# Two places in TensorE's order: a score ahead of the last stack transposes, and a score between the halves of the values

## Chip, core and metric

One core of a Trainium2 chip. The metric is the device time of one execution in microseconds (us). The kernel before takes 53.62 us, the median of 3 runs (53.51 to 53.62).

## What is computed

The input x is (2, 128, 16, 16): two batches, 128 channels, 256 positions. A recurrent layer over the channels comes first, then an attention layer over 256 tokens of 128 features, and a table-like layer at the end. The change concerns the attention:

```python
qkv = jnp.einsum('bsh,oh->bso', x, w_qkv)
qkv = qkv.reshape(batch, seq_len, 3, nh, hd)          # 8 heads of 16
q, k, v = jnp.transpose(qkv, (2, 0, 3, 1, 4))
attn = jnp.einsum('bhqd,bhkd->bhqk', q, k) / math.sqrt(hd)
pos = jnp.arange(seq_len)[None, :] - jnp.arange(seq_len)[:, None]
bias = jnp.where(pos <= 0, pos.astype(jnp.float32) * math.log(RECENCY_DECAY), jnp.zeros((), dtype=jnp.float32))
attn = jax.nn.softmax(attn + bias[None, None, :, :], axis=-1)
out = jnp.einsum('bhqk,bhkd->bqhd', attn, v).reshape(batch, seq_len, hidden)
return jnp.einsum('bsh,oh->bso', out, w_out) + b_out
```

## The kernel before

Each engine runs an order written out by hand; semaphores join them. There are 2 batches of 8 heads, which makes 16 heads h, in 4 groups g of 4 heads. Steps named here are functions of the same name in the blocks of the engines.

**Stacks.** Queries and keys are split into high and low f16 parts, duplicated, and transposed on TensorE by `transpose_stacks(g)` (eight 128x128 transposes, L935). They go to one bank of PSUM (bank 6 for groups 2 and 3), and ScalarE (`even_stacks(g)`, L488) and VectorE (`odd_stacks(g)`, L668) copy them out. `transpose_stacks(3)` waits until both have copied group 2.

**Maxima.** `scores_by_query(h)` (L963) makes the scores of head h with queries on the partitions, two f16 matmuls of 128x256, into one of two banks in turn. VectorE's `largest(h)` (L761) takes their maxima, and after the fourth head of a group writes them as two f16 parts (L768, L769). `scores_by_query(h)` waits until `largest(h - 2)` is over. `shift_rows(g)` (L977) transposes the parts, and `even_shifts(g)` on ScalarE (L492) and `odd_shifts(g)` on VectorE (L672) put them into rows of the stacks.

**Probabilities and values.** `scores_by_key(h)` (L994 and L996, four matmuls) makes the shifted scores with keys on the partitions. ScalarE's `exponentials(c)` (L511) takes two heads at once. `values(g, t)` (L1013) multiplies the probabilities of the four heads of a group by the values, for half t of the keys: eight f32 records of 128x32 with 256 columns, one head beside the other in the array, and half 1 adds to half 0. Both halves wait for `exponentials(2g + 1)`. Values(0) and values(1) wait for more: values(0) until stacks 3 are copied out of the bank, values(1) for `by_query(0)`. Half 1 releases VectorE.

**Normalisation.** VectorE transposes the result (`by_query(g)`, L679), inverts the sums (`invert(g)`, L683), GpSimd multiplies (L352), VectorE transposes back (`by_dim(g)`, L687), and TensorE projects (`project(b)`, L1029). VectorE's order around the change is: largest(5), odd_stacks(2), largest(6), largest(7), odd_stacks(3), largest(8), odd_shifts(1), largest(9), by_query(0), largest(10), invert(0), largest(11), largest(12), by_dim(0), odd_shifts(2), largest(13), by_query(1), invert(1), largest(14), by_dim(1), largest(15), residual(0). ScalarE's is even_stacks(2), exponentials(0), even_stacks(3), exponentials(1), even_shifts(1), exponentials(2), exponentials(3), even_shifts(2), and so on.

TensorE's own order stands at the end of its block; behind the loop come project(0), shift_rows(3), values(2, 0) and (2, 1), four scores by key, values(3, 0) and (3, 1), and the tail.

Of the kernel before, what the change touches and what calls it, by code (L numbers as in the profile page):

```python
# [23 lines left out]
HG = 4  # L24
# [17 lines left out]
def conv_attn_ffn(nc, x, log_A, dt_w, dt_b, ln_w, ln_b, w_qkv, w_out, b_out, out):  # L42
# [3 lines left out]
    with ExitStack() as ctx:  # L46
# [781 lines left out]
        def _(pe):  # L828
# [94 lines left out]
            def transpose_stacks(g):  # L923

                b = g // 2
                pe.wait_ge(s_dup, HALVES * (b + 1))
                pe.wait_ge(s_hi1, HALVES)
                if g >= 2:
                    pe.wait_ge(s_even0 if g == 2 else s_even, 2)
                    pe.wait_ge(s_odd0 if g == 2 else s_odd, 2)  # L930
                for o in range(2):
                    for a in range(2):
                        for t in range(HALVES):
                            h = HG * (g % 2) + 2 * a
                            last = pe.transpose(stacks_ps[g][:, o, a, P * t:P * (t + 1)],  # L935
                                                parts[:, 2 * b + t, o, h:h + 2, :, :]
                                                .rearrange("p h i d -> p (h i d)"), ident16[:])
                last.then_inc(s_stacks, 1)
# [10 lines left out]
            def scores_by_query(h):  # L949

                b, e = h // HEADS, h % HEADS
                if h < HG:
                    pe.wait_ge(s_even0, h // 2 + 1)
                    pe.wait_ge(s_odd0, h // 2 + 1)
                else:
                    pe.wait_ge(s_even, h // HG)
                    pe.wait_ge(s_odd, h // HG)
                if h == 0:
                    pe.wait_ge(s_pad, 7)
                if h >= 2:  # L960
                    pe.wait_ge(s_max, h - 1)
                for t in range(HALVES):
                    last = pe.matmul(s1_ps[h % 2][:, HW * t:HW * (t + 1)],  # L963
                                     qT[:, e, HW * b + P * t:HW * b + P * (t + 1)],
                                     kT[:, e, HW * b:HW * (b + 1)], start=True, stop=True)
                last.then_inc(s_s1, 1)

            def shift_rows(g):

                pe.wait_ge(s_mp, g + 1)  # L970
                if g == 0:
                    pe.wait_ge(s_woT, 1)
                else:
                    pe.wait_ge(s_mre, g)
                    pe.wait_ge(s_mro, g)
                for t in range(HALVES):
                    last = pe.transpose(mT_ps[:, P * t:P * (t + 1)],  # L977
                                        mparts[:, g, t, :, :].rearrange("p h w -> p (h w)"), ident16[:])
                last.then_inc(s_mT, 1)

            def scores_by_key(h):

                c, b, e = h // 2, h // HEADS, h % HEADS
                pe.wait_ge(s_mre if h % 2 == 0 else s_mro, h // HG + 1)
                if h % 2 == 0:
                    if c >= 2:
                        pe.wait_ge(s_exp, c - 1)
                    else:
                        pe.wait_ge(s_lo, HALVES * (c + 1))
                        pe.wait_ge(s_v, HALVES * (c + 1))  # L990
                        pe.wait_ge(s_consts, 2)
                for t in range(HALVES):
                    dst = s2_ps[c % 2][:, h % 2, HW * t:HW * (t + 1)]
                    pe.matmul(dst, kT[:, e, HW * b + P * t:HW * b + P * (t + 1)], qT[:, e, HW * b:HW * (b + 1)],  # L994
                              start=True, stop=False)
                    last = pe.matmul(dst[:, P * t:HW], ident16[:], qmk[:, 0:HW - P * t], start=False, stop=True)  # L996
                if h % 2 == 1:
                    last.then_inc(s_s2, 1)

            def values(g, t):  # L1000

                b = g // 2
                if g == NG - 1:
                    pe.wait_ge(s_mre, NG)
                    pe.wait_ge(s_mro, NG)
                elif g > 0:
                    pe.wait_ge(s_pvq, g)
                else:
                    pe.wait_ge(s_odd, NG - 1)
                    pe.wait_ge(s_even, NG - 1)  # L1010
                pe.wait_ge(s_exp, 2 * g + 2)
                for j in range(HG):
                    last = pe.matmul(pv_ps[g][VW * j:VW * (j + 1), :],  # L1013
                                     v_aug[:, 2 * b + t, HG * (g % 2) + j, :], probs[:, HG * g + j, t, :],
                                     start=(t == 0), stop=(t == HALVES - 1))
                if t == HALVES - 1:
                    last.then_inc(s_pv, 1)
# [62 lines left out]
            scores_by_key(0)  # L1080
            scores_by_key(1)
            scores_by_query(6)
            scores_by_key(2)
            transpose_stacks(3)
            scores_by_query(7)
            scores_by_key(3)
            for g in range(2, NG):
                scores_by_query(HG * g)
                shift_rows(g - 1)
                scores_by_query(HG * g + 1)  # L1090
                values(g - 2, 0)
                values(g - 2, 1)
                scores_by_query(HG * g + 2)
                scores_by_key(HG * g - 4)
                scores_by_key(HG * g - 3)
                scores_by_query(HG * g + 3)
                scores_by_key(HG * g - 2)
                scores_by_key(HG * g - 1)
# [42 lines left out]
```

## Time and profile before

| | |
|---|---|
| median of 3 runs | 53.62 us (53.51 to 53.62) |
| the profiled execution | 53.42 us |
| its span in the profile | 51.7 us |
| busy in the span: TensorE | 40.9 us (79%) |
| VectorE | 40.2 us (78%) |
| ScalarE | 28.6 us (55%) |
| GpSimd | 23.5 us (45%) |
| the chain that ended last: TensorE, VectorE, GpSimd, ScalarE | 35%, 24%, 13%, 10% of the span |

A row of the timeline gives the start from the span's beginning and the duration in us, the engine (PE is TensorE's matmuls, DVE VectorE, ACT ScalarE, POOL GpSimd), the line, the operation, what it writes and reads with shapes, and how many instructions are merged; in brackets stands the idle time of the engine before it, and what ended it. The chain of work that ended last is followed back from the last instruction; "issue" in it is time in which nothing in the profile explains the wait. Matmuls overlap: the distance of two starts is what one takes from the engine, and the recorded duration is longer.

### The profile page before, as it was taken

How to read it: one execution, taken by the hardware profiler on the slowest of the kernel's cores; microseconds unless marked ns; L12 is line 12 of the kernel's file. 1: busy time of each engine (PE TensorE's matmuls, PEld its weight loads, DVE VectorE, ACT ScalarE, POOL GpSimd, SP SyncE). 2: the span in 40 equal slices, each digit the busy share in tenths (PEclk: the TensorE clock that was granted, in tenths of full speed). 3: DMA queues.
4: the chain of work that ended last, by engine and by line, in shares of the span. 5: the costliest groups of instructions: out<-in, count | busy, mean ns of one | idle time of the engine just before them, and what ended most of it. 6: DMA issues, size and time to landing. Idle time of an engine off the chain costs nothing.

```text
span 51.7 us, 1021 instructions
## 1 busy us (share of the span) xinstructions
PE 40.9 (79%) x310; PEld 26.3 (51%) x312; DVE 40.2 (78%) x135; ACT 28.6 (55%) x63; POOL 23.5 (45%) x64
## 2 busy tenths in 40 slices
PE   0999899999996859649957996999994596996700
PEld 0332789685442645429824682599482352842500
DVE  2799778848983599999889999989999954699520
ACT  3600656395476768967998079339649900056020
POOL 4789432099999989736950031040029204016000
PEclk9999995569999999999999999999999999999999
DMA  0392400000000000000000000000000000002002
GB/s 0 80 304 42 35 5 0 0 0 0 0 0 6 0 0 0 0 6 13 6 0 0 0 0 0 0 13 0 0 0 0 0 0 0 0 0 101 1 0 101
DMA packets 1565, 0.92 MB, mean 18 GB/s; under 512 B 404, under 2 KB 1560, under 8 KB 1560
## 3 DMA queue, kind: packets, MB, share of 16 engines
q1 hardware_dynamic: 1104, 0.79, 4.9%
q10 hardware_dynamic: 456, 0.08, 1.7%
q8 instruction: 2, 0.03, 0.3%
q14 instruction: 3, 0.02, 0.2%
HBM read 0.60 MB, written 0.26 MB: 17 GB/s over the span
## 4 chain that ended last, share of the span: by engine, by line
PE 35%; DVE 24%; POOL 13%; ACT 10%; issue 7%; DMA 6%; POOLq 0%; DVEq 0%
PE ps L1013 8%; ACT probs L511 8%; DMA x_sb<-in_x_dram 6%; PE ps L994 5%; PE ps L963 4%; POOL stacks L303 4%; DVE negmax L761 4%; POOL stacks L304 4%; PE ps L996 4%; PE ps L935 3%; PE ps L1029 3%; PE ps L859 2%; POOL parts L310 2%; PE ps L913 2%; POOL wc L298 2%
## 5 line engine op out<-in xcount | busy, mean ns | idle before, releaser
L761 DVE TENSOR_REDUCE negmax<-ps 128x2 f32<-128x512 f32 x16 | 10.7, 675 | 0.8 <-PE ps L963 0.6
L511 ACT ACTIVATE probs<-ps 128x1024 f32<-128x1024 f32 x8 | 8.0, 1021 | 3.9 <-PE ps L996 3.9
L833 PE MATMUL ps<-warm 128*128 128x512 bf16 x28 | 8.9, 452 | 1.4 <-DVE warm L556 1.3
L994 PE MATMUL ps<-stacks 128*128 128x256 f16 x32 | 7.0, 273 | 0.0
L352 POOL TENSOR_TENSOR on<-pvq,rsum 128x256 f32<-128x256 f32 x3 | 1.8, 616 | 10.7 <-DVE rsum L683 10.7
L996 PE MATMUL ps<-qmk,ident 128*128 128x256 f16 (+1 forms) x32 | 6.6, 246 | 0.0
L963 PE MATMUL ps<-stacks 128*128 128x256 f16 x32 | 6.0, 274 | 0.2 <-ACT stacks L485 0.2
L833 PEld LDWEIGHTS ps<-warm 128*128 128x128 bf16 x30 | 3.2, 113 | 5.0 <-issue 2.2
L1013 PE MATMUL ps<-probs,v_aug 128*32 128x256 f32 x64 | 4.3, 384 | 1.7 <-ACT probs L511 1.5
L913 PE MATMUL ps<-wT,xtT 128*128 128x384 f32 x8 | 3.2, 505 | 0.7 <-ACT xtT L437 0.6
L994 PEld LDWEIGHTS ps<-stacks 128*128 128x128 f16 x32 | 3.1, 98 | 0.8 <-ACT stacks L492 0.4
L1013 PEld LDWEIGHTS ps<-probs,v_aug 128*32 128x32 f32 x64 | 1.9, 108 | 3.1 <-issue 2.0
L963 PEld LDWEIGHTS ps<-stacks 128*128 128x128 f16 x32 | 2.5, 97 | 2.0 <-issue 1.3
L996 PEld LDWEIGHTS ps<-qmk,ident 128*128 128x128 f16 x32 | 3.1, 98 | 0.2
L498 ACT ACTIVATE fln<-fmv 128x2 f32<-128x2 f32 x2 | 0.4, 203 | 5.1 <-DVE fmv L712 5.1
L488 ACT COPY stacks<-ps 64x1024 f16<-64x1024 f16 x3 | 3.0, 1005 | 0.3 <-PE ps L935 0.3
L935 PE MATMUL ps<-ident,parts 128*128 128x128 f16 x32 | 2.3, 219 | 0.8 <-POOL parts L310 0.8
L1029 PE MATMUL ps<-woutT,oT 128*128 128x128 f32 x16 | 2.5, 289 | 0.4 <-DVE oT L687 0.4
L1029 PEld LDWEIGHTS ps<-woutT,oT 128*128 128x128 f32 x16 | 2.0, 191 | 1.3 <-issue 1.3
L935 PEld LDWEIGHTS ps<-ident,parts 128*128 128x128 f16 x32 | 1.8, 97 | 1.6 <-issue 1.0
L977 PE MATMUL ps<-ident,mparts 128*128 128x128 f16 x8 | 1.1, 224 | 1.8 <-DVE mparts L769 1.8
L687 DVE STREAM_TRANSPOSE oT<-on 128x256 f32<-128x256 f32 x4 | 1.8, 443 | 0.9 <-POOL on L360 0.7
(159 smaller groups left out, 94.4 us busy)
## 6 DMA issues: line engine op xcount, KB each, us to landing
x_sb<-in_x_dram SPq DMA_DIRECT2D x1, 256.0 KB, 2.9
out_dram<-y_sb SPq DMA_DIRECT2D x2, 128.0 KB, 1.7
wqkv_sb<-in_L_attn_w_qkv_dram SPq DMA_DIRECT2D x1, 192.0 KB, 3.0
wout_sb<-in_L_attn_w_out_dram SPq DMA_DIRECT2D x1, 64.0 KB, 3.3
bout_bc<-in_L_attn_b_out_dram ACTq DMA_DIRECT2D x1, 64.0 KB, 3.8
params<-in_L_conv_ln_w_dram ACTq DMA_DIRECT2D x1, 1.0 KB
params<-in_L_conv_ln_b_dram ACTq DMA_DIRECT2D x1, 1.0 KB
params<-in_L_conv_dt_w_dram ACTq DMA_DIRECT2D x1, 0.5 KB
```

The lines of the kernel that those rows point to most:

```text
L303: link(pool.memset(kv[row:row + 2, :, a, e, :].bitcast(F32), SHIFT_PAIR), s=s_pad)
L488: act.copy(group_stacks(g, 0)[0:P // 2], stacks_ps[g][0:P // 2]).then_inc(s_even, 1)
L511: act.activation(probs[:, 2 * c:2 * c + 2, :, :].rearrange("p h k q -> p (h k q)"), s2_ps[c % 2].rearrange("p a n -> p (a n)"), ACT.Exp, s ...
L761: dve.tensor_reduce(negmax[:, g, :, quadrant], s1_ps[h % 2].rearrange("p (q k) -> p q k", q=HALVES), AX_X, ALU.max, negate=True).then_inc( ...
L833: pe.matmul(ps[:, bank, :], warm[:, 0:P], warm[:], start=True, stop=True)
L913: pe.matmul(qkv_ps[:, t, 0:3 * P], xtT[:, P * t:P * (t + 1)], wT[:, 0:3, :].rearrange("p k h -> p (k h)"), start=True, stop=True).then_inc ...
L935: last = pe.transpose(stacks_ps[g][:, o, a, P * t:P * (t + 1)], parts[:, 2 * b + t, o, h:h + 2, :, :] .rearrange("p h i d -> p (h i d)"), ...
L963: last = pe.matmul(s1_ps[h % 2][:, HW * t:HW * (t + 1)], qT[:, e, HW * b + P * t:HW * b + P * (t + 1)], kT[:, e, HW * b:HW * (b + 1)], sta ...
L994: pe.matmul(dst, kT[:, e, HW * b + P * t:HW * b + P * (t + 1)], qT[:, e, HW * b:HW * (b + 1)], start=True, stop=False)
L996: last = pe.matmul(dst[:, P * t:HW], ident16[:], qmk[:, 0:HW - P * t], start=False, stop=True)
L1013: last = pe.matmul(pv_ps[g][VW * j:VW * (j + 1), :], v_aug[:, 2 * b + t, HG * (g % 2) + j, :], probs[:, HG * g + j, t, :], start=(t == 0), ...
L1029: last = pe.matmul(proj_ps[b][:, t, :], oT[:, 2 * b + g, P * t:P * (t + 1)], woutT[:, g, :], start=(g == 0), stop=(g == 1), skip_group_che ...
```

## The change

Two moves in TensorE's order, and nothing else. The score of head 7 goes ahead of the score by key of head 2 and of the last stack transposes. In the loop, for g = 2 and g = 3, the third score of group g (heads 10 and 14) goes between the two halves of the values of group g - 2.

```diff
             scores_by_key(0)
             scores_by_key(1)
             scores_by_query(6)
+            scores_by_query(7)
             scores_by_key(2)
             transpose_stacks(3)
-            scores_by_query(7)
             scores_by_key(3)
             for g in range(2, NG):
                 scores_by_query(HG * g)
                 shift_rows(g - 1)
                 scores_by_query(HG * g + 1)
                 values(g - 2, 0)
+                scores_by_query(HG * g + 2)
                 values(g - 2, 1)
-                scores_by_query(HG * g + 2)
                 scores_by_key(HG * g - 4)
                 scores_by_key(HG * g - 3)
                 scores_by_query(HG * g + 3)
```

## Rows read from the trace of the kernel before

**Rows 1.** Busy time by stage: us, PE, PEld, DVE, ACT, POOL, granted clock, DMA.
```profile
27.90:32.25 4.35, 3.87 (x42) 2.57 (x43) 4.28 (x11) 2.52 (x4) 0.62 (x1) 1.00 0.00 0
32.25:36.60 4.35, 4.34 (x46) 3.33 (x47) 3.96 (x11) 2.48 (x3) 0.62 (x1) 1.00 0.01 4
```

**Rows 2.** The chain that ended last: start, us, what.
```profile
32.12 0.14 issue
...
35.40 0.95 PE ps L1029 x8
```

**Rows 3.** Timeline of TensorE's matmuls: start, us, what, idle time before.
```profile
24.65 0.27 PE L994 MATMUL ps<-stacks 128*128 128x256 f16 x1
...
25.12 0.61 PE L935 MATMUL ps<-ident,parts 128*128 128x128 f16 x8
...
27.91 1.07 PE L1013 MATMUL ps<-probs,v_aug 128*32 128x256 f32 x16 [0.22 <-DVE stacks L668]
28.91 0.39 PE L963 MATMUL ps<-stacks 128*128 128x256 f16 x2
29.14 0.27 PE L994 MATMUL ps<-stacks 128*128 128x256 f16 x1
...
29.52 0.27 PE L994 MATMUL ps<-stacks 128*128 128x256 f16 x1
...
36.33 0.28 PE L977 MATMUL ps<-ident,mparts 128*128 128x128 f16 x2
...
40.67 1.07 PE L1013 MATMUL ps<-probs,v_aug 128*32 128x256 f32 x16 [1.35 <-ACT probs L511]
```

**Rows 4.** Timeline of ScalarE: copy of stacks 3, an exponential, two exponentials.
```profile
25.77 1.01 ACT L488 COPY stacks<-ps 64x1024 f16<-64x1024 f16 x1
26.68 1.02 ACT L511 ACTIVATE probs<-ps 128x1024 f32<-128x1024 f32 x1
...
34.46 2.01 ACT L511 ACTIVATE probs<-ps 128x1024 f32<-128x1024 f32 x2 [1.74 <-PE ps L996]
```

**Rows 5.** Timeline of VectorE.
```profile
24.25 0.69 DVE L668 COPY stacks<-ps 64x1024 f16<-64x1024 f16 x1
...
25.98 0.69 DVE L761 TENSOR_REDUCE negmax<-ps 128x2 f32<-128x512 f32 x1 [0.32 <-PE ps L963]
...
27.16 0.69 DVE L668 COPY stacks<-ps 64x1024 f16<-64x1024 f16 x1
...
28.82 0.68 DVE L761 TENSOR_REDUCE negmax<-ps 128x2 f32<-128x512 f32 x1
29.42 0.43 DVE L679 STREAM_TRANSPOSE pvq<-ps 128x256 f32<-128x256 f32 x1
...
32.71 0.67 DVE L761 TENSOR_REDUCE negmax<-ps 128x2 f32<-128x512 f32 x1
33.39 0.45 DVE L679 STREAM_TRANSPOSE pvq<-ps 128x256 f32<-128x256 f32 x1
...
36.08 0.20 DVE L769 SCALAR_TENSOR_TENSOR mparts<-negmax,mparts 128x8 f16<-128x8 f32 x1
...
41.87 0.45 DVE L679 STREAM_TRANSPOSE pvq<-ps 128x256 f32<-128x256 f32 x1 [0.46 <-PE ps L1013]
```

**Rows 6.** Timeline of GpSimd: the product of group 1.
```profile
34.16 0.62 POOL L352 TENSOR_TENSOR on<-pvq,rsum 128x256 f32<-128x256 f32 x1 [2.92 <-DVE rsum L683]
```

**Rows 7.** Timeline of TensorE in narrow windows, where the array's shape changes.
```profile
32.90 0.43 PE L1013 MATMUL ps<-probs,v_aug 128*32 128x256 f32 x4
...
33.26 0.39 PE L963 MATMUL ps<-stacks 128*128 128x256 f16 x2
...
44.40 0.39 PE L1044 MATMUL ps<-ident,t 128*128 128x128 f32 x2
44.72 0.28 PE L1052 MATMUL ps<-ident,eq 128*32 128x128 f16 x2
```

**Rows 8.** The page: granted TensorE clock in 40 slices of the span.
```profile
PEclk9999995569999999999999999999999999999999
```

## Prediction

> **What bounds the kernel now.** I read the table by stage first [rows 1], then the chain of work that ended last [rows 2], then the timelines of the three engines in the stretch that the change touches [rows 3 to 7]. In the two stages that hold the halved values, from 27.90 to 36.60, VectorE is busy 4.28 and 3.96 of 4.35 us each, TensorE 3.87 and 4.34, ScalarE 2.52 and 2.48 [rows 1]. So no engine alone is the bound; the order is. The chain says which: odd stacks 27.16, values(0) 27.91, a score, four scores by key, two exponentials that end at 32.12, values(1) at 32.26, the same again, then project(0) from 35.40, shift_rows(3) and values(2) [rows 2, 3]. That ring (values, a score, scores by key, exponentials, 4.35 us from 27.91 to 32.26) sets the pace, and each piece put into it between values and the keys lengthens every later step.
>
> Three things meet at its end. Shift_rows(3) starts at 36.33, just behind project(0), which ends at 36.35 (35.40 + 0.95), and 0.05 behind the last part of the maxima, which VectorE ends at 36.28 (36.08 + 0.20); the exponentials of the group end at 36.47 (34.46 + 2.01) [rows 2 to 5]. A gain needs all three earlier; a loss on one is a loss. The path to 36.28 on VectorE is by_query(1) at 33.39, the inverse, GpSimd's product from 34.16 to 34.78, by_dim(1), largest(15) and the two parts of the maxima [rows 5, 6]. So by_query(1) sets shift_rows(3), and by_query(1) needs the *whole* of values(1). They end at 33.33 (32.90 + 0.43) [rows 7], VectorE's largest(13) at 33.38 (32.71 + 0.67) [rows 5]. There is 0.05 us of slack.
>
> **Part one: the eighth score ahead.** Score 7 only needs largest(5), over before VectorE's next operation at 24.25 [rows 5], so it doesn't wait behind score 6. Its two matmuls take the engine for 0.22 (the 0.23 from 28.91 to 29.14 hold 0.01 of what lies ahead), key 2 goes out from 24.87 instead of 24.65 for 0.38 (29.14 to 29.52 for a like one) [rows 3], and the last stack transposes start at 25.25 instead of 25.12: 0.13 later and not 0.22, since before they waited for stacks(2), copied at 24.94 (24.25 + 0.69) [rows 3, 5]. They take 0.61 and end at 25.86 rather than 25.73 [rows 3]. Key 3 loses nothing: the same work lies ahead of it.
> The gain: score 7 is done at 25.03 (24.65 + 0.38), so VectorE loses its idle 0.32, starts largest(7) at 25.69 instead of 25.98, and all behind it is 0.29 earlier; odd_stacks(3) ends at 27.56 instead of 27.85 [rows 5].
> The price: ScalarE's even_stacks(3) begins at 25.77, 0.04 after the transposes' end, and its exponential follows at 26.68 with no idle time between [rows 4]. It now begins at 25.90, its exponential at 26.81, and that ends at 27.83 instead of 27.70. Values(0) wait for both: TensorE follows ScalarE's exponential by 0.14 (32.12 to 32.26) [rows 2], so ScalarE now releases them at 27.97, where VectorE did at 27.91 [rows 3]. The 0.29 buys nothing at this point, and the ring begins **0.06 later**. Bounds: -0.29 if ScalarE's copy doesn't slip and its exponential weren't the gate; +0.15 if the whole 0.22 of the score reached it (27.70 + 0.22 + 0.14 = 28.06). I take +0.06, since the queue of ScalarE is seen full.
>
> **Part two: a score between the halves of values.** Nothing is added or removed; score 10 (and 14) moves ahead of values(g, 1). Its own wait is no matter: largest(8) is over when largest(9) starts, at 28.53 (28.82 less 0.29) [rows 5], and values(0, 0) last longer. What changes is the shape of the array twice more per group. Values are 128x32 matmuls, four heads side by side, in four batches of four; scores are 128x128. The batches follow by 0.21 (32.26 to 32.90 for three), but the score behind the last batch starts 0.36 after it (32.90 to 33.26) [rows 3, 7]. That start is 0.07 before the last record's end. The same 0.07 stands at a turn the other way in the tail: the 128x128 records end at 44.79 (44.40 + 0.39), the 128x32 ones start at 44.72 [rows 7]. So I price each turn as "last record's end less 0.07".
> One half of values: 0.21 + 0.43 - 0.07 = 0.57. The pair of a score between two turns: 0.39 - 0.07 = 0.32, instead of 0.23 (28.91 to 29.14). Values, score and values again: 0.57 + 0.32 + 0.57 = 1.46 until the first score by key, against 1.23 now (27.91 to 29.14) [rows 3]: **+0.23 per group** on the ring. And values of a group are complete 0.57 + 0.32 + 0.21 + 0.43 = 1.53 after their start instead of 1.07: **+0.46** for by_query. Bounds of the ring's term: 0 if a turn costs nothing more than it does now (then by_query is still 0.22 later, by the score's own time); -0.22 if the score vanished under the values; +0.37 if each turn waited for the record's whole end.
> The Trainium skill, "TensorEngine Tiling (Array Packing)", Key Properties, says that a change of the tiling mode, not of the tile alone, drains TensorE. That speaks against this edit, and the rows of the two turns bear it out but for the 0.07. Read to the letter (wait for the end of the record), it would put the time some 0.3 us above my forecast (0.14 more on the ring of group 0 and 0.14 more until the values of group 1 are complete).
>
> **The sum.** Group 0: values from 27.97, complete at 29.50. VectorE is through largest(9) at 29.21 (29.50 less 0.29) and now idles. An idle VectorE starts 0.13 after the values' end (41.74 to 41.87) [rows 3, 5], so by_query(0) is at 29.63 instead of 29.42: the 0.29 gained has turned into 0.21 lost. Largest(10), for which score 10 was moved, stands *behind* by_query(0) in VectorE's order, so its early score is not used. Largest(11), the parts of the maxima, shift_rows(2) and score 13 follow 0.21 later, until 32.31, and are hidden: values(1) don't start before 32.26 + 0.06 + 0.23 = 32.55.
> Group 1: values(1) complete at 32.55 + 1.53 = 34.08, by_query(1) at 34.21 instead of 33.39, **+0.82**. VectorE idles from 33.59 to 34.21. Everything on the path to shift_rows(3) moves by that, to 37.15. The rivals for that place come earlier: the exponentials end at 36.47 + 0.06 + 0.46 = 36.99, and project(0), which would start its first pair some 0.5 later and find the transposed values of group 1 0.82 later, loses part of that wait behind the first pair and ends ahead of 37.15. Behind shift_rows(3) the order is unchanged; values(2), their exponentials, values(3) at 40.67 and the tail move as one [rows 3]. VectorE's side work of the tail (it had 0.46 idle before its last by_query [rows 5]) moves by the same 0.82 and stays beside.
> The profiled execution took 53.42 (its span 51.7), so the sum is 54.24 against that; the median of the runs shown is 53.62, 0.20 above. On the median's footing: 53.62 + 0.82 = 54.44; I say **54.4**.
>
> **The rivals.** *Cheap turns.* If two more turns cost nothing, the ring has only +0.06, by_query(1) gets 0.06 + 0.22 for the score ahead of half the values + 0.07 for VectorE's slower start from idle = +0.35: 53.97. For it: the turns seen are few, and matmul ends are modelled. Against: the 0.36 instead of 0.21 is a distance of starts, and stands alike in all groups.
> *Not slower: the score fills the drain.* The 0.15 behind the last batch might take in other work, so that the score between costs less than its own time. With a term t per group, by_query(1) moves by 0.35 + 2t; it decides at t = -0.18. At t = -0.22, the score wholly hidden, the result is -0.09: 53.53. Against it: the score that follows values today does not start under them.
> *Clock.* The granted clock is at its upper level, 2.4 GHz, in every slice behind the front part, through an idle time of 1.35 us of TensorE [rows 3, 8], and the longest new idle is shorter. A slice at 5 (1.2 GHz), as there are two in the front part, would slow the matmuls in it and give a time above the range; it gets the small rest.
>
> **How the numbers follow.** Chances: forecast 0.62 (54.2 to 54.65), cheap turns 0.21 (53.75 to 54.2), not slower 0.13 (half of it within 0.2%, half faster), the rest 0.04 above. Range 53.75 to 54.65, which leaves out the not slower case and the clock. A measurement of this kernel can't tell less than about 0.2% from nothing (0.11 us). Faster 0.06, same 0.08, slower 0.86.
>
> **What would show it.** Part one: largest(7) without idle time, odd_stacks(3) ending near 27.56, even_stacks(3) at 25.90, and values(0) released by the exponential at 27.97. Part two: score 10 0.57 after values(0, 0), values(0, 1) 0.32 after score 10, the key score 1.46 after the start; by_query(0) and (1) with idle time before them, (1) at 34.21, with 0.6 us of it. Shift_rows(3) near 37.15 with VectorE as releaser. I am wrong if values(g, 1) start 0.22 after the score, or if by_query(1) comes within 0.1 of 33.39, or if the tail takes back part of the 0.82.

## The result

The changed kernel is slower. Against the kernel before, which ran beside it (53.56 us median of 8 executions), the ratio is 1.0124 with a 95% interval of 1.0094 to 1.0154, that is +0.66 us (0.50 to 0.82). A second measurement gave 1.0113 (1.0069 to 1.0157). Forecast were 54.4 us and +0.82; on 53.56 the ratio gives 54.22.

Four of the changed kernel's eight executions (55.32 to 55.77 us, the others 54.01 to 54.30) and one of the eight of the kernel before (54.96) were of a slower kind, which the ratio leaves out, and the profiled execution of the changed kernel is among them (55.42 us, span 53.7): it lost 1.31 us in the front part, ahead of everything that the change touches. So times are taken from an event in front of the change, the anchor: the third stack transposes (eight matmuls of L935, `transpose_stacks(2)`). They start at 23.21 before and at 24.52 after, so 1.31 comes off every time of the changed kernel. Two rows from the timeline of the kernel before, the anchor and the last instruction:

```profile
23.21 0.62 PE L935 MATMUL ps<-ident,parts 128*128 128x128 f16 x8 [0.27 <-POOL parts L310]
...
49.28 0.29 DVE L825 COPY y_sb<-ps 128x128 f32<-128x128 f32 x1 [0.61 <-PE ps L1052]
```

The same two in the timeline of the changed kernel, and between them TensorE's rows that answer to [rows 3]:

```profile
24.52 0.62 PE L935 MATMUL ps<-ident,parts 128*128 128x128 f16 x8 [0.27 <-POOL parts L310]
...
26.57 0.61 PE L935 MATMUL ps<-ident,parts 128*128 128x128 f16 x8
...
29.28 0.64 PE L1013 MATMUL ps<-probs,v_aug 128*32 128x256 f32 x8 [0.61 <-ACT probs L511]
29.85 0.39 PE L963 MATMUL ps<-stacks 128*128 128x256 f16 x2
30.18 0.64 PE L1013 MATMUL ps<-probs,v_aug 128*32 128x256 f32 x8
30.75 0.28 PE L994 MATMUL ps<-stacks 128*128 128x256 f16 x1
...
33.88 0.64 PE L1013 MATMUL ps<-probs,v_aug 128*32 128x256 f32 x8 [0.23 <-ACT probs L511]
34.45 0.39 PE L963 MATMUL ps<-stacks 128*128 128x256 f16 x2
34.77 0.64 PE L1013 MATMUL ps<-probs,v_aug 128*32 128x256 f32 x8
...
38.43 0.28 PE L977 MATMUL ps<-ident,mparts 128*128 128x128 f16 x2
38.64 1.07 PE L1013 MATMUL ps<-probs,v_aug 128*32 128x256 f32 x16
...
51.28 0.29 DVE L825 COPY y_sb<-ps 128x128 f32<-128x128 f32 x1 [0.58 <-PE ps L1052]
```

From anchor to last row it is 26.07 before (49.28 - 23.21) and 26.76 after: **+0.69**, within the interval of the timed ratio. Some 0.03 of such an end is not the change's: VectorE's wait in front of its last copy is 0.61 in the kernel before and in one of the variants below, and 0.58 in all the other timelines of this document. Without it the change costs some 0.72, as at the start of values(2). Values(0) now wait for ScalarE's exponential and no longer for VectorE's copy. Values, score and values last until the first score by key 1.47 (29.28 to 30.75), against 1.23 in [rows 3].

ScalarE in the changed kernel, against [rows 4], and VectorE, against [rows 5]:

```profile
27.21 1.00 ACT L488 COPY stacks<-ps 64x1024 f16<-64x1024 f16 x1
28.12 1.02 ACT L511 ACTIVATE probs<-ps 128x1024 f32<-128x1024 f32 x1
```

```profile
26.28 1.29 DVE L761 TENSOR_REDUCE negmax<-ps 128x2 f32<-128x512 f32 x2
...
28.15 0.69 DVE L668 COPY stacks<-ps 64x1024 f16<-64x1024 f16 x1
...
30.88 0.45 DVE L679 STREAM_TRANSPOSE pvq<-ps 128x256 f32<-128x256 f32 x1 [0.40 <-PE ps L1013]
...
35.48 0.45 DVE L679 STREAM_TRANSPOSE pvq<-ps 128x256 f32<-128x256 f32 x1 [0.56 <-PE ps L1013]
...
38.18 0.19 DVE L769 SCALAR_TENSOR_TENSOR mparts<-negmax,mparts 128x8 f16<-128x8 f32 x1
```

Less 1.31, the copy of the stacks starts at 25.90 (0.13 later), VectorE's copy at 26.84 (0.32 earlier), by_query(0) at 29.57 (0.15 later) and by_query(1) at 34.17 (0.78 later). VectorE gained 0.32 and then stood idle twice, 0.40 and 0.56, for the whole of the values.

Shift_rows(3) start at 37.12 (38.43 less 1.31), against 37.15 in the forecast, and the chain that ended last reaches them as forecast: by_query(1), the inverse, GpSimd's product, by_dim(1), largest(15), then the two parts of the maxima, of which these are its last pieces:

```profile
38.18 0.21 DVE mparts L769
38.38 0.05 issue
38.43 0.28 PE ps L977 x2
```

### The profile page after: what moved, and what is told of

Read it like the earlier page. It is cut to its first block, busy times and chain, and to the rows that moved or that the text cites. A ratio compares the mean times of both kernels' runs of the same rounds, so it can differ in the third digit from the quotient of the medians.

```text
span 53.7 us, 1021 instructions
## 1 busy us (share of the span) xinstructions
PE 42.5 (79%) x310; PEld 26.6 (49%) x312; DVE 40.4 (75%) x135; ACT 28.6 (53%) x63; POOL 23.5 (44%) x64
## 4 chain that ended last, share of the span: by engine, by line
PE 47%; DVE 22%; ACT 16%; issue 6%; POOL 4%; DVEq 0%
PE ps L833 10%; ACT probs L511 9%; PE ps L1013 9%; PE ps L913 5%; DVE negmax L761 4%; PE ps L963 4%; PE ps L994 3%; PE ps L935 3%; PE ps L996 2%; PE ps L882 2%; ACT stacks L488 2%; DVE pvq L679 2%; DVE oT L687 2%; PE ps L859 2%; POOL parts L310 2%
## 5 line engine op out<-in xcount | busy, mean ns | idle before, releaser
L833 PE MATMUL ps<-warm 128*128 128x512 bf16 x28 | 9.8, 485 | 1.5 <-DVE warm L556 1.3
L935 PE MATMUL ps<-ident,parts 128*128 128x128 f16 x32 | 2.3, 219 | 0.8 <-POOL parts L310 0.8
L679 DVE STREAM_TRANSPOSE pvq<-ps 128x256 f32<-128x256 f32 x4 | 1.8, 450 | 1.4 <-PE ps L1013 1.4
L310 POOL COPY parts<-parts 128x256 f16<-128x256 f16 x4 | 1.6, 397 | 2.5 <-DVE parts L649 1.4
L935 PEld LDWEIGHTS ps<-ident,parts 128*128 128x128 f16 x32 | 1.8, 97 | 1.5 <-issue 1.0
```

What stands on the lines that cost most here:

```text
L679: dve.transpose(pvq[:, g, :, :].rearrange("p a w -> p (a w)"), pv_ps[g]).then_inc(s_pvq, 1)
L833: pe.matmul(ps[:, bank, :], warm[:, 0:P], warm[:], start=True, stop=True)
```

## The experiments

All kernels ran beside the kernel before. In the table each time is a start in the kernel's own timeline, counted from its third stack transposes, less the same for the kernel before, in us; the timed ratio stands with its 95% interval. For the two kernels that were profiled twice the starts repeat to about 0.01 us; the last instruction can move by 0.03, as said above. "Halved" means that a score stands between the two halves of the values.

| kernel | values(0) | by_query(0) | values(1) | by_query(1) | values(2) | last instruction | timed ratio |
|---|---|---|---|---|---|---|---|
| changed, again | +0.06 | +0.15 | +0.31 | +0.78 | +0.71 | +0.69 | 1.0113 (1.0069 to 1.0157) |
| score 7 ahead alone | +0.07 | -0.32 | +0.06 | +0.07 | +0.07 | +0.05 | 0.9978 (0.9957 to 0.9999); again 1.0005 (0.9978 to 1.0032) |
| both halvings alone | 0.00 | +0.32 | +0.48 | +0.95 | +0.89 | +0.89 | 1.0148 (1.0108 to 1.0187) |
| only group 0 halved | 0.00 | +0.32 | +0.48 | +0.48 | +0.48 | +0.44 | 1.0069 (1.0039 to 1.0099) |
| only group 1 halved | 0.00 | 0.00 | 0.00 | +0.47 | +0.41 | +0.38 | 1.0078 (1.0049 to 1.0106) |
| stacks ahead of key 2 | -0.07 | -0.31 | -0.07 | -0.07 | -0.07 | -0.09 | 0.9968 (0.9942 to 0.9995) |
| changed, stacks ahead | -0.07 | +0.02 | +0.17 | +0.64 | +0.58 | +0.56 | 1.0098 (1.0060 to 1.0136) |
| changed, maxima first | +0.07 | +0.28 | +0.31 | +0.79 | +0.72 | +0.70 | 1.0129 (1.0083 to 1.0174) |
| score 14 ahead of values | -0.07 | -0.32 | +0.17 | +0.18 | +0.12 | +0.10 | 0.9993 (0.9965 to 1.0021) |

**The changed kernel again.**

> The changed kernel once more, for its timeline beside the parts. The theory of the prediction: ScalarE's exponential releases values(0) 0.06 us later than before; each split adds 0.23 us ahead of the scores by key and completes the values 0.46 later; by_query(1) is 0.75 to 0.82 later than before, and the kernel 0.7 slower. The rival of cheap turns: values to scores by key 1.23 us as before, by_query(1) +0.35, kernel +0.35.

It repeats the first timeline to 0.01 us. The rival of cheap turns is out: neither 1.23 to the keys nor +0.35 at by_query(1).

**Only the score of head 7 ahead.**

```diff
             scores_by_query(6)
+            scores_by_query(7)
             scores_by_key(2)
             transpose_stacks(3)
-            scores_by_query(7)
```

> Only the score of head 7 moved ahead; values whole. Theory: largest(7) to largest(9) 0.29 us earlier, but the last stack transposes, ScalarE's copy and its exponential 0.13 later, values(0) 0.06 later, and by_query(1) 0.06 to 0.13 later: kernel +0.06 to +0.13 us. Rival (VectorE paces this stretch, so its 0.29 reach the end): kernel 0.1 to 0.29 us faster.

The first measurement hinted at a gain that the timeline doesn't have. So the same kernel ran a second time:

> Only the score of head 7 ahead, a second time, because its timed runs (ratio 0.998) and its timeline (0.07 us later from values(0) on, 0.04 at the end) point opposite ways. If the timeline is right, the ratio is between 1.000 and 1.002; if the move has a gain that the compared stretch doesn't show, it is again 0.998 or less.

The ratio was 1.0005. The timeline's +0.05 us would be 1.0009: the second interval holds it, the first ends 0.0010 below. Once more 0.07 later from values(1) on in its timeline, the move has no gain; and a single interval that ends just below 1 is no proof of one here. VectorE's 0.32 is there in by_query(0), and it is gone at by_query(1), which waits for values(1) and not for VectorE.

**Only the halved values, in both groups.**

```diff
                 values(g - 2, 0)
+                scores_by_query(HG * g + 2)
                 values(g - 2, 1)
-                scores_by_query(HG * g + 2)
```

> Only the halved values, in both groups; score of head 7 where it was. Theory: +0.23 us on the ring in group 0, values(1) complete 0.23 + 0.46 later, by_query(1) +0.69, less 0.07 that shift_rows(3) had to spare behind the exponentials: kernel +0.62. Rival of cheap turns: by_query(1) +0.22, kernel +0.15 to +0.22.

More than expected, by 0.26 at by_query(1) and 0.27 at the end. TensorE's timeline of this kernel says why:

```profile
27.88 0.64 PE L1013 MATMUL ps<-probs,v_aug 128*32 128x256 f32 x8 [0.22 <-DVE stacks L668]
28.70 0.38 PE L963 MATMUL ps<-stacks 128*128 128x256 f16 x2 [0.18 <-DVE negmax L761]
29.01 0.64 PE L1013 MATMUL ps<-probs,v_aug 128*32 128x256 f32 x8
```

Score 10 needs largest(8). Without the first part of the change largest(8) ends 0.3 later, and the score, now ahead of half 1, waits with both behind it. The second half starts 1.13 after the first instead of the 0.90 of the changed kernel. So the two parts of the change aren't independent: the first costs 0.06 itself and saves the second this wait of 0.23, 0.17 net (+0.89 against +0.71 to +0.72 at values(2)).

**One group at a time.**

```diff
                 values(g - 2, 0)
+                if g == 2:
+                    scores_by_query(HG * g + 2)
                 values(g - 2, 1)
-                scores_by_query(HG * g + 2)
+                if g != 2:
+                    scores_by_query(HG * g + 2)
```

> Only the values of group 0 halved, around the score of head 10. Theory: the ring is 0.23 us longer, values(1) and by_query(1) 0.23 later, VectorE's by_query(0) up to 0.4 later but caught up by group 1: kernel +0.17 to +0.23. Cheap turns: 0 to +0.05. If by_query(0)'s delay reached the end through VectorE: +0.4.

With 3 in the place of 2:

> Only the values of group 1 halved, around the score of head 14. Theory: values(1) complete 0.46 us later, by_query(1) +0.46, kernel +0.39 (0.07 to spare behind the exponentials). Rival (the ring alone counts, VectorE has time to spare): +0.23. Cheap turns: +0.15 to +0.22.

Group 1 alone came as worked out: by_query(1) +0.47, values(2) +0.41. Group 0 alone gave +0.48 where 0.17 to 0.23 were expected, by the same wait for largest(8). All of it comes through the ring: by_query(0)'s +0.32 has no part in it, since values(1) start with the exponentials. Together they make 0.48 + 0.41 = 0.89, which is the sum for both.

**A turn of the array's shape by itself.** One matmul more between the halves of values(3), where TensorE has nothing else to do. With the full array's shape:

```diff
             values(3, 0)
+            pe.matmul(ps[:, 2, 0:HW], warm[:, 0:P], warm[:, 0:HW], start=True, stop=True)
             values(3, 1)
```

> The kernel before with one more matmul between the halves of the last values, values(3), where nothing else competes: 128x128 weights, 256 columns, its result unused. Theory (a turn of the array's shape starts 0.07 us before the last record's end): half 1 starts 0.57 + 0.20 = 0.77 after half 0 instead of 0.43, kernel +0.34 us. Cheap turns: +0.11, the streaming of 256 columns.

And with the values' own shape, at the same 256 columns:

```diff
             values(3, 0)
+            pe.matmul(ps[0:VW, 2, 0:HW], warm[:, 0:VW], warm[:, 0:HW], start=True, stop=True)
             values(3, 1)
```

> As the run with the additional 128x128 matmul between the halves of values(3), but with 128x32 weights, so the shape of the array doesn't change; the same 256 columns. Theory: no turn, so +0.05 to +0.15 us for the columns alone. If the cost were that of any foreign matmul between the halves: +0.34 as there.

TensorE's timeline of the first, then of the second:

```profile
42.17 0.64 PE L1013 MATMUL ps<-probs,v_aug 128*32 128x256 f32 x8 [1.35 <-ACT probs L511]
42.74 0.28 PE L1106 MATMUL ps<-warm 128*128 128x256 bf16 x1
42.96 0.64 PE L1013 MATMUL ps<-probs,v_aug 128*32 128x256 f32 x8
43.53 0.71 PE L1029 MATMUL ps<-woutT,oT 128*128 128x128 f32 x4
```

```profile
40.67 0.64 PE L1013 MATMUL ps<-probs,v_aug 128*32 128x256 f32 x8 [1.35 <-ACT probs L511]
41.10 0.27 PE L1106 MATMUL ps<-warm 128*32 128x256 bf16 x1
41.14 0.67 PE L1013 MATMUL ps<-probs,v_aug 128*32 128x256 f32 x8
41.74 0.71 PE L1029 MATMUL ps<-woutT,oT 128*128 128x128 f32 x4
```

From the first half to the projection it is 1.36 and 1.07; before it was 1.00. The same 256 columns cost 0.36 in the other shape and 0.07 in the same one. Not all of the 0.29 between them is turns: in a stream 256 columns take 0.11 (a score's two matmuls 0.22), so in the values' shape the foreign matmul went partly beside the others, and 0.04 of the 0.29 are columns that are hidden there. The two turns are 0.36 - 0.11 = 0.25: 0.14 on the way out (0.57 from the half to the foreign matmul, where two batches take 0.43) and 0.11 on the way back (0.22 for 0.11). Each start behind a turn is again 0.07 (0.06 once) before the last record's end. Half 1 starts 0.79 after half 0, where 0.77 was expected.

The weight loads (PEld) show where a part of it goes. Across a turn, in the first run, the load starts with the turn and with its own matmul; in the same shape, in the second, 0.21 ahead of its matmul (40.89 and 41.10):

```profile
42.74 0.10 PEld L1106 LDWEIGHTS ps<-warm 128*128 128x128 bf16 x1 [0.41 <-issue]
```

```profile
40.89 0.09 PEld L1106 LDWEIGHTS ps<-warm 128*32 128x32 bf16 x1
```

The last instruction is 0.43 and 0.16 later than before, but 0.09 of each is there from the fourth stack transposes on, far ahead of the added matmul: in both kernels these start 2.00 after the anchor, in the kernel before 1.91, with the same work ahead of them. No other kernel here has that shift, and its cause stays open. Behind it 0.34 and 0.07 are left, for 0.34 and 0.05 to 0.15 expected. The timed ratios are 1.0149 (0.9971 to 1.0327) and 1.0003 (0.9974 to 1.0032); the first is too wide to tell, and the verdict rests on the timelines.

**The stack transposes ahead of the score by key.** Score 7 early, but nothing more between the copy's end and the transposes:

```diff
             scores_by_query(6)
-            scores_by_key(2)
-            transpose_stacks(3)
             scores_by_query(7)
+            transpose_stacks(3)
+            scores_by_key(2)
             scores_by_key(3)
```

> The kernel before with the score of head 7 ahead, and the last stack transposes straight behind it, the score by key of head 2 behind them; values whole. Theory: the transposes keep their start (they wait for the copy of group 2 anyhow), ScalarE isn't delayed, its exponential releases values(0) 0.07 us earlier than VectorE's copy does now, and the whole ring follows: kernel -0.07 us. Rival (VectorE's 0.29 count): -0.2 or more. If the score ahead is what delays ScalarE: +0.06 as with the score alone.

In the timeline it is 0.07 ahead of the kernel before from values(0) to values(2), 0.09 at the last instruction, of which up to 0.03 may be the chance named above. Timed it is 0.9968 (0.9942 to 0.9995), measured once: an interval like the first one of the score alone, which a second measurement didn't confirm. So the gain is as sure as the timeline makes it, and no surer. TensorE:

```profile
24.40 0.60 PE L963 MATMUL ps<-stacks 128*128 128x256 f16 x4
25.09 0.61 PE L935 MATMUL ps<-ident,parts 128*128 128x128 f16 x8
...
27.80 0.42 PE L1013 MATMUL ps<-probs,v_aug 128*32 128x256 f32 x4 [0.46 <-ACT probs L511]
```

The transposes keep their time, so ScalarE isn't late, and its exponential releases values(0) 0.07 earlier than VectorE's copy did. VectorE is 0.31 ahead, of which 0.24 buy nothing.

The same order in the changed kernel:

> The changed kernel with the last stack transposes straight behind the score of head 7. Theory: only ScalarE's 0.13 us comes back, and the ring passes it on whole: values(0) 0.07 earlier than before the change instead of 0.06 later, kernel 0.13 faster than the changed kernel, some 0.5 to 0.6 slower than before. Rival (VectorE's waits swallow it): as the changed kernel.

Everything from values(0) to the end came 0.13 to 0.14 earlier than in the changed kernel (+0.58 against +0.71 at values(2)). A shift on ScalarE in front of values(0) is passed on whole.

**The early scores used.** In the changed kernel, VectorE's order:

```diff
-            by_query(0)
             largest(10)
+            by_query(0)
...
+            largest(14)
             by_query(1)
             invert(1)
-            largest(14)
```

> The changed kernel with VectorE's order altered so that the early scores are used: largest(10) ahead of by_query(0), largest(14) ahead of by_query(1). Theory: VectorE's idle time is filled, but by_query(1) now waits for largest(14) and comes 0.15 to 0.2 later than in the changed kernel: kernel +0.15 to +0.2 on it. Rival (the split was right and only VectorE's order wastes it): faster than the changed kernel by 0.3 or more.

Neither happened: by_query(1) is at +0.79, as in the changed kernel. Its timeline of VectorE:

```profile
34.54 1.33 DVE L761 TENSOR_REDUCE negmax<-ps 128x2 f32<-128x512 f32 x2
35.78 0.44 DVE L679 STREAM_TRANSPOSE pvq<-ps 128x256 f32<-128x256 f32 x1
...
37.19 0.45 DVE L687 STREAM_TRANSPOSE oT<-on 128x256 f32<-128x256 f32 x1 [0.73 <-POOL on L352]
```

Largest(14) fits just into the time that VectorE would have waited, and the time it leaves further back is spent waiting for GpSimd's product, which hangs on by_query(1). I had expected 0.15 to 0.2 of delay because I put largest(14)'s end too late. That the scores are early has no worth in either order; that the values are late has its whole price in both.

**The other way round: score 14 in front of values(1).** On top of the version with the stacks ahead:

```diff
+                if g == 3:
+                    scores_by_query(HG * g + 2)
                 values(g - 2, 0)
                 values(g - 2, 1)
-                scores_by_query(HG * g + 2)
+                if g != 3:
+                    scores_by_query(HG * g + 2)
```

> The version with the stack transposes ahead of the score by key of head 2, and the score of head 14 in front of values(1) instead of behind them, values whole: the pieces stay outside both the halves and the stretch to the scores by key, but values(1) wait for the score. Theory: values(1) start 0.10 us later than before, the first score by key behind them 0.13 earlier; by_query(1), which needs the values' end, 0.10 later, and it sets the end: kernel 0 to +0.05 us against before, 0.1 slower than with the stacks ahead alone. Rival (the ring of exponentials alone counts): 0.13 to 0.2 faster than before.

The exponentials of group 2 do gain on values(1) (exponentials(4) start at -0.05, although values(1) are at +0.17), but by_query(1) at +0.18 sets shift_rows(3), and values(2) are at +0.12. Values(1) were delayed by 0.24 on the version it starts from, not by the 0.17 expected: score 14 had a wait for largest(12) in front (0.17 of idle time) and takes 0.31 to the values behind it, with its turn. The mechanism held; the size was off. Timed it is not told from the kernel before (0.9993, 0.9965 to 1.0021).

## Why the prediction was right, and where it wasn't

**Part one** came as worked out. Stack transposes +0.13, copy +0.13, values(0) released by ScalarE at +0.06. VectorE's gain was 0.32, not 0.29: in a row of maxima the second starts before the first one's recorded end (two take 1.29 in the row above). That this gain doesn't reach the end was right and is shown by the run with this part alone.

**Part two, the turns.** Half 0.57, score 0.32 to 0.33, half 0.57: the rows give 1.47 for the forecast's 1.46, so +0.24 per group on the ring for +0.23; from half 0's start to the end of half 1 it is 1.54 (29.28 to 30.82) for 1.53. The rule of the two turns seen in the trace before held in each of the new ones, and the two runs with a foreign matmul show that the shape is the cause: in the values' own shape it costs 0.07. They don't part the drain itself from the weight load that starts only with the turn. The Trainium skill's rule ("TensorEngine Tiling (Array Packing)", Key Properties), that a change of tiling mode drains TensorE, agrees with these rows: 0.25 for two turns. Read to the letter, up to the record's end, it was too dear by 0.07 a turn.

**The wait of score 10.** "Its own wait is no matter" was right for the whole change, but the text gave no price for the cover. The run without part one has it: 0.17 at the end of the ring. It is the one thing that part one buys.

**By_query(1).** Forecast +0.82, measured +0.78. The missing 0.04 are a term that I sized by the wrong row, less 0.02 that the ring came later: I let an idle VectorE start 0.13 after the values' end, by the last by_query [rows 5]. Behind values(0) and values(1) it started 0.06 and 0.07 after it (30.82 to 30.88, 35.41 to 35.48), after idle times of 0.40 and 0.56, while the last one had only 0.46. So idle time doesn't set that latency; what makes the last one slower stays open.

**Behind shift_rows(3)** I let all move as one. That was the second mis-sized term, 0.07: before, values(2) waited for the exponentials (36.47 + 0.14 = 36.61), not for shift_rows(3). Now shift_rows(3) moved by 0.79 and values(2) start 0.21 behind it instead of 0.28, which is the turn again (0.28 - 0.07 = 0.21). I had named the three that meet there, and then counted only one of them. It makes +0.71 to +0.72 of +0.78. This is one of the signs of being wrong that the forecast named, that a part of the 0.82 is taken back behind shift_rows(3), and it came. The forecast of 0.82 was 0.13 above the timeline's 0.69: 0.04, 0.07, and 0.02 to 0.03 that the last instruction's chance makes. Both mis-sized terms erred to the same side, so the total isn't right by errors that cancel.

**The rivals.** Cheap turns: excluded, by the halves' starts and the foreign matmul. The score filling the drain: excluded, it starts 0.57 after the half. The clock: the granted clock stayed at its upper level in all slices behind the front, in the changed kernel too; only the last slice reads 6. The page of the changed kernel, and that of its second profile:

```profile
PEclk9999996555589999999999999999999999999996
```

```profile
PEclk9999999999999999999999999999999999999999
```

The front holds more slices at 5 (1.2 GHz) than in [rows 8], ahead of the change; the two stages that it lengthens have the full clock in both kernels. The second profile has the upper level in every slice and the same starts behind the anchor to 0.01, so the clock has no part in the +0.69.

## What to carry to other kernels

Where an engine computes in two array shapes, count the turns in a proposed order, and read their price from a turn that the trace already has (here the last record's end less 0.07 us): a score put between two halves cost 0.24 us on the ring, and made the values complete 0.47 later, though no work was added. Ask who uses the thing that comes early and who waits for the thing that comes late: here the maxima had no use for an early score, and the transposition of the values, on which three engines hang, needed both halves. And when a step moves ahead of another, look at what the other's consumer has queued: the gain of 0.32 on VectorE was spent at ScalarE, whose full queue got its work 0.13 late; the stack transposes moved ahead turned that into 0.07 us of gain in the timeline.

## What the runs showed of the hardware

A 128x32 matmul of 256 columns, put between two halves of four such matmuls side by side, held the next half back by 0.04 us only (41.10 to 41.14) and the projection by 0.07, though 256 columns take 0.11 in a stream: work in the same shape partly goes beside the others. In the full array's shape, the same one took 0.22 between its start and the next half's (42.74 to 42.96), besides the 0.14 of the turn in front of it. Two turns cost 0.25 together, and weights of the other shape were not loaded before the turn (42.74, with the matmul), where weights of the same shape were loaded 0.21 ahead (40.89 to 41.10).
